# Attention scores as products of 64 rows, two at a time in the halves of the array

## Chip, cores and metric

The kernel runs on one core of a Trainium2 chip. The metric is the time of one execution on the device in microseconds (us); the median of three runs stands for a kernel. The span of a profiled execution is the time from its first to its last instruction.

## What is computed

Two layers on float32 inputs. The change touches the first layer's attention: 8 sequences of 512 tokens, width 256, 16 heads of 16.

```python
qkv = jnp.einsum('bsd,hde->bhse', x, Wqkv) + bqkv[None, :, None, :]   # x: layer norm of the input, (8, 512, 256)
q, k, v = jnp.split(qkv, 3, axis=-1)
score = jnp.einsum('bhsd,bhtd->bhst', q, k)
score = jnp.where(causal[None, None], score, -jnp.inf)
attn = jax.nn.softmax(score / jnp.sqrt(HEAD_DIM), axis=-1)
out = jnp.einsum('bhst,bhtd->bhsd', attn, v)   # then transposed to (b, s, d)
out = out @ Wout + bout
```

After it come a mixture of nine experts (one of them shared), a gated scan and a second mixture, which the change leaves as they are. Their weights and loops are not shown.

## The kernel before

`mix_phase` does the first attention and the router of the experts, one batch (a sequence, 512 tokens) after the other, 8 in all; `experts_phase` and `layer1_phase` follow it. Each engine has its own instruction list, in which waits on semaphores are written by hand: `pe` (TensorE), `dve` (VectorE), `act` (ScalarE), `pool` (GpSimd), and `sp` (SyncE, which issues nearly all DMAs). An engine works its list strictly in the order written, and a DMA that SP issues stands behind all waits that SP has before it.

**Precision.** Products are made of float16 parts: x is split into a high and a low part, and a product is hi*hi + hi*lo + lo*hi (`three_products`, L143). For the scores the three are stacked along the contraction: `q_stack` and `k_stack` (L197, L198) hold for each head 16 rows of (hi, hi), 16 of (hi, lo) and 16 of (lo, hi), in partitions 0 to 47. Rows 48 to 95 are zero (cleared once, `clear`), and row 96 holds minus the row's maximum on the q side and ones on the k side. The stacks are filled through DRAM: ACT and DVE make `qk_hi` and `qk_lo` with (head, dimension) on the partitions, SP stores them (L350, L359), and once they have landed fetches them back as 16 rows by heads (`fetch_heads`, L372 to L376, six DMAs of 128 KB a half batch). Two sets of stacks alternate by batch.

**Two passes over the scores.** The *q pass* (`scores_q`, L908) has a block of 128 queries on the output's partitions and the keys along it; a mask product (identity times `mask_qk`, L925) puts -1e30 above the diagonal; DVE reduces each unit to minus its row maximum (`maxima`, L752). A group is four heads; its work is cut into 11 units (`A_UNITS`, L78) of up to 512 columns, which go through two banks in turn. When a group is through, DVE turns its 128x32 block of maxima (`turn_maxima`, L761) and ACT sends it with four small DMAs into row 96 of `q_stack` (`load_max`, L540). The *k pass* (`scores_k`, L927) has keys on the partitions and queries along it, over 97 rows, so that the maximum comes off in the product; ACT takes the exponential (L537), POOL clears above the diagonal (L452), and the value products (L955, float32, four heads side by side in strips of 32 columns of the array) sum over keys.

**Order.** The loop over s (head 0 to 127 through all batches) and n (0 to 2) gives each engine one slot per (s, n). A slot of PE has: the k pass of head s+1 part n, one q unit of the group two ahead (`LEAD`), and in named slots other work: values, transposes, the projections of the next batch, the output projection of the last (`AT_...`, L90 to L95). The slot number within a batch is at = 3h + n (0 to 47), within a group i = at mod 12. The k pass of a group begins at i = 9 of the group before (s+1 is a multiple of 4 at i = 9) and waits for `max_loaded` (L933); the q units wait for `stacks_loaded` at at = 24 (first half of the next batch) and at = 0 (second half).

## Time and profile before

| | us |
|---|---|
| median of 3 timed runs | 1208.96 |
| lowest, highest | 1206.2, 1209.35 |
| span of the profiled execution | 1206.9 |
| attention stage (first q product of batch 0 to the last k products) | 28.8 to 446.5 |
| a batch in the middle of it | 51.44 |

The profile is of one execution. The page gives the totals of each engine; the views below cut the stretch of the attention out of it. TensorE's time has two kinds of row: PE (products; their ends are modelled, so the distance of two starts says more than a length) and PEld (weight loads).

### The profile page before, as it was taken

How to read it: one execution, taken by the hardware profiler on the slowest of the kernel's cores; microseconds unless marked ns; L12 is line 12 of the kernel's file. 1: busy time of each engine (PE TensorE's matmuls, PEld its weight loads, DVE VectorE, ACT ScalarE, POOL GpSimd, SP SyncE). 2: the span in 40 equal slices, each digit the busy share in tenths (PEclk: the TensorE clock that was granted, in tenths of full speed). 3: DMA queues.
4: the chain of work that ended last, by engine and by line, in shares of the span. 5: the costliest groups of instructions: out<-in, count | busy, mean ns of one | idle time of the engine just before them, and what ended most of it. 6: DMA issues, size and time to landing. Idle time of an engine off the chain costs nothing. (4 is left out here: it accounts for less than half of the span.)

```text
span 1206.9 us, 26712 instructions
## 1 busy us (share of the span) xinstructions
PE 1111.1 (92%) x8873; PEld 745.7 (62%) x8905; DVE 897.4 (74%) x2217; ACT 676.1 (56%) x1463; POOL 529.1 (44%) x743
## 2 busy tenths in 40 slices
PE   4789999999999987998999999996999999999998
PEld 2345555555455546887999888983656646546555
DVE  5778887888888757975766657775876877877876
ACT  2256565555556564565656656664654664664653
POOL 5443434334243235844444444423646547447414
PEclk9689999999999999999999999998999999999999
DMA  5538544354533404665232453452241331331211
GB/s 146 112 67 237 102 80 98 80 111 96 93 81 80 99 19 155 215 179 165 79 127 83 119 163 124 126 149 85 89 141 36 106 126 48 105 102 64 96 45 62
DMA packets 105044, 129.36 MB, mean 107 GB/s; under 512 B 14976, under 2 KB 92736, under 8 KB 103936
## 3 DMA queue, kind: packets, MB, share of 16 engines
q1 hardware_dynamic: 93952, 109.27, 33.8%
q0 software_dynamic: 6912, 18.88, 5.6%
q8 instruction: 46, 0.75, 0.3%
q10 hardware_dynamic: 4096, 0.14, 0.2%
q14 instruction: 38, 0.31, 0.1%
HBM read 84.70 MB, written 43.38 MB: 106 GB/s over the span
## 5 line engine op out<-in xcount | busy, mean ns | idle before, releaser
L537 ACT ACTIVATE p<-bank 128x384 f32<-128x384 f32 (+1 forms) x384 | 191.9, 530 | 186.4 <-PE bank L937 118.8
L757 DVE TENSOR_REDUCE neg_max<-bank 128x1 f16<-128x384 f32 (+3 forms) x352 | 219.7, 640 | 64.7 <-PE bank L925 56.4
L452 POOL TENSOR_SCALAR_AFFINE_SELECT p<-p 128x256 f32<-128x256 f32 x256 | 104.1, 410 | 247.3 <-ACT p L537 246.7
L922 PE MATMUL bank<-k_stack,q_stack 96*128 96x384 f16 (+3 forms) x512 | 133.5, 313 | 20.1 <-DVE neg_max L757 13.1
L1377 POOL DMA_INDIRECT fetched<-xn_dram,token_now x80 | 81.2, 1015 | 42.8 <-POOL token_now L1373 30.6
L937 PE MATMUL bank<-q_stack,k_stack 97*128 97x512 f16 (+1 forms) x256 | 91.5, 362 | 6.0 <-ACT p L537 3.5
L2006 POOL TENSOR_TENSOR up_lo<-up_sq,up_hi 128x512 f16<-128x512 f32 x32 | 43.9, 1399 | 120.7 <-ACT up_hi L2063 120.7
L2017 POOL TENSOR_TENSOR he_lo<-he_sq,he_hi 128x512 f16<-128x512 f32 x64 | 79.9, 1268 | 36.7 <-ACT he_hi L2106 36.6
L1461 ACT ACTIVATE a<-xbank,b 128x256 f32<-128x256 f32 (+1 forms) x126 | 58.6, 468 | 51.2 <-PE xbank L149 47.8
L1549 DVE TENSOR_TENSOR h_lo<-h,h_hi 128x256 f16<-128x256 f32 x159 | 68.4, 433 | 24.4 <-ACT h_hi L1470 23.5
L955 PE MATMUL bank<-p,v_aug 128*32 128x512 f32 (+3 forms) x1024 | 83.5, 445 | 0.8 <-DVE o_rows L737 0.8
L147 PE MATMUL ybank<-l_xT_hi,pack_hi 128*128 128x512 f16 x208 | 78.9, 379 | 4.9 <-DVE up_sq L2220 2.5
L922 PEld LDWEIGHTS bank<-k_stack,q_stack 96*128 96x128 f16 x512 | 45.0, 99 | 59.4 <-DVE neg_max L757 40.9
L1468 ACT ACTIVATE h<-prod 128x256 f32<-128x256 f32 x159 | 64.9, 408 | 26.3 <-DVE prod L1543 21.2
L149 PE MATMUL ybank<-l_xT_hi,pack_lo 128*128 128x512 f16 x208 | 78.8, 379 | 0.0
L148 PE MATMUL ybank<-l_xT_lo,pack_hi 128*128 128x512 f16 x208 | 78.8, 379 | 0.0
L925 PE MATMUL bank<-mask_qk,identb 128*128 128x128 bf16 (+1 forms) x321 | 76.9, 240 | 0.0
L1543 DVE SCALAR_TENSOR_TENSOR prod<-xbank,b,a 128x256 f32<-128x256 f32 (+1 forms) x126 | 58.4, 477 | 24.0 <-ACT a L1461 19.3
L147 PE MATMUL ybank<-pack_hi,up_hi 128*128 128x256 f16 x256 | 69.8, 273 | 0.0
L148 PE MATMUL ybank<-pack_lo,up_hi 128*128 128x256 f16 x256 | 69.8, 273 | 0.0
L149 PE MATMUL ybank<-pack_hi,up_lo 128*128 128x256 f16 x256 | 69.8, 273 | 0.0
L1991 POOL DMA_INDIRECT rows_k<-y_routed_dram,slot x56 | 56.5, 1008 | 27.7 <-issue 15.9
(342 smaller groups left out, 3375.2 us busy)
## 6 DMA issues: line engine op xcount, KB each, us to landing
w_bc<-wT_dram SPq DMA_DIRECT2D x8, 2048.0 KB, 8.0
y_routed_dram<-y SPq DMA_DIRECT2D x37, 256.0 KB
w<-in_w SPq DMA_DIRECT2D x10, 704.0 KB, 6.9
pack<-in_pack SPq DMA_DIRECT2D x12, 342.0 KB, 4.1
xr<-in_x SPq DMA_DIRECT2D x8, 512.0 KB, 7.3
xn_dram<-xn SPq DMA_DIRECT2D x8, 512.0 KB, 3.1
qk_hi_dram<-qk_hi SPq DMA_DIRECT2D x16, 256.0 KB, 2.4
qk_lo_dram<-qk_lo SPq DMA_DIRECT2D x16, 256.0 KB, 2.4
```

The costliest lines, as they stand in the source:

```text
L147: pe.matmul(out, hi_a(c), hi_b(c), start=first and x == 0, stop=False)
L148: pe.matmul(out, hi_a(c), lo_b(c), start=False, stop=False)
L149: mm = pe.matmul(out, lo_a(c), hi_b(c), start=False, stop=last and x == n - 1)
L452: pool.affine_select(out=diagonal, in_=diagonal, pattern=[[0, 2], [1, P]], compare_op=ALU.is_ge, fill=0.0, base=0, channel_multiplier=-1). ...
L537: act.activation(p32[:, s // GH % 2, s % GH, cols], s_bank[n][:, 0:cols.stop - cols.start], ACT.Exp).then_inc(p_exp.sem, 1)
L757: dve.tensor_reduce(neg_max[:, g % 2, 0:GH * TT].rearrange("p (h t) -> p h t", t=TT)[:, heads[0]:heads[-1] + 1, j], a_bank[c % 2][:, 0:len ...
L922: pe.matmul(to[:, at * w:(at + 1) * w], q_stack[0:STK, u, h0 + h, j * P:(j + 1) * P], k_stack[0:STK, u, h0 + h, 0:w], start=at == 0, stop= ...
L925: pe.matmul(diagonal, identb[:, :], mask_qk[:, 0:len(heads), :], start=False, stop=True).then_inc(a_psum.sem, 1)
L937: mm = pe.matmul(to[:, 0:S - n * P], k_stack[0:AUG, u, h, n * P:(n + 1) * P], q_stack[0:AUG, u, h, n * P:S], start=True, stop=True)
L955: mm = pe.matmul(out_bank[VW * h:VW * (h + 1), k * P:S], v_aug[:, b % 2, k, GH * (g % NG) + h, :], p32[:, g % 2, h, P_OFF[k]:P_OFF[k] + S ...
L1377: pool.indirect_dma_start(fetched[:, u, half, :], None, dram["xn"], bass.IndirectOffsetOnAxis(token_now[:, u, half:half + 1], 0)).then_inc ...
L2017: pool.tensor_tensor(he_lo[:, e, :], he_sq[:, e % EB, :], he_hi[:, e, :], ALU.subtract).then_inc(he_lo_s.sem, 1)
```

## The change

- The stacks have 48 rows (49 with the maximum) instead of 96 (97). Even heads stand in partitions 0 to 48, odd heads in 64 to 112; one tile column holds a pair of heads. The products of both passes so use the upper or the lower 64 rows. Clearing goes away; `free` holds the place of the memory saved.
- A q unit is of one parity (`par`) and one or two pairs. There are 12 units per group, one in each slot. In slot (s, n) the unit's parity is s mod 2 and that of the k pass is (s+1) mod 2.
- The mask is made of two products over 64 rows (`mask_rows`, `mask_cols`), one for each half of the 128 columns of a diagonal block, in the same rows of the array as the unit. POOL makes these masks in 13 small instructions at the start.
- DVE turns the maxima of a group one slot later, at i = 0, after that slot's reduction.
- SP sends the maxima, eight DMAs per group (four for each parity) instead of ACT's four; each has its place in SP's list, and the fetches, stores and loads behind it wait for it.
- DRAM holds the stacked order: SP stores each high part twice and each low part once (six DMAs of 128 KB a half batch, before two of 256 KB), and fetches 48 rows at once (four DMAs of 192 KB, before six of 128 KB).

```diff
-STK, AUG = 96, 97
+STK, AUG = 48, 49
+HI_SLOTS, LO_SLOTS = ((0, 2), (1, 2)), ((1,), (0,))
+HALF = 64
+HEAD_PAIRS = NH // 2
...
-A_UNITS = (((0, 1, 2, 3), 0), ((0, 1), 1), ((2, 3), 1), ((0,), 2), ((1,), 2), ((2,), 2), ((3,), 2),
-           ((0,), 3), ((1,), 3), ((2,), 3), ((3,), 3))
+A_UNITS = ((0, (0, 1), 1), (0, (0, 1), 0), (0, (0,), 2), (1, (0, 1), 1), (1, (0, 1), 0), (1, (0,), 2),
+           (0, (0,), 3), (0, (1,), 3), (0, (1,), 2), (1, (0,), 3), (1, (1,), 3), (1, (1,), 2))
...
-AT_MAX = {0: (0, 1), 1: (2, 3)}
...
-        q_stack = sb("q_stack", [AUG, 2, NH, S], F16)
-        k_stack = sb("k_stack", [AUG, 2, NH, S], F16)
+        q_stack = sb("q_stack", [P, 2, HEAD_PAIRS, S], F16)
+        k_stack = sb("k_stack", [P, 2, HEAD_PAIRS, S], F16)
+        free = sb("free", [P, 2, NH, S], F16)
...
+            def store_slots(of, half, places):
+
+                for a, slots in enumerate(places):
+                    for r in slots:
+                        to = dram["qk"][a, half * NH // 2:(half + 1) * NH // 2, r]
+                        sp.dma_start(to, of[:, 2 * a + half, :]).then_inc(qk_stored.sem, 16)
+
             def store_hi(b, half):
-                hi_rows = dram["qk_hi"].rearrange("(a m p) s -> p m a s", a=2, p=P)[:, half]
-                hi_tile = qk_hi[:, :, :].rearrange("p (a m) s -> p m a s", a=2)[:, half]
                 sp.wait_ge(qk_hi_s.sem, qk_hi_s.at(b, 2 * half + 2))
-                sp.dma_start(hi_rows, hi_tile).then_inc(qk_stored.sem, 16)
-
-            def load_stacks(b, half):
-
-                u, heads = b % 2, slice(half * NH // 2, (half + 1) * NH // 2)
-                lo_rows = dram["qk_lo"].rearrange("(a m p) s -> p m a s", a=2, p=P)[:, half]
-                lo_tile = qk_lo[:, :, :].rearrange("p (a m) s -> p m a s", a=2)[:, half]
+                store_slots(qk_hi, half, HI_SLOTS)
+
+            def store_lo(b, half):
                 sp.wait_ge(q_lo_s.sem, q_lo_s.at(b, half + 1))
                 sp.wait_ge(k_lo_s.sem, k_lo_s.at(b, half + 1))
-                sp.dma_start(lo_rows, lo_tile).then_inc(qk_stored.sem, 16)
+                store_slots(qk_lo, half, LO_SLOTS)
...
+            def load_max(g):
+
+                b, pair0 = g // NG, GH // 2 * (g % NG)
+                sp.wait_ge(max_rows_s.sem, max_rows_s.at(g))
+                for par in range(2):
+                    row = HALF * par + STK
+                    for q in range(4):
+                        to = q_stack[row:row + 1, b % 2, pair0:pair0 + GH // 2, :].rearrange("o h (t q c) -> o q h t c", t=TT, q=4)[:, q]
+                        at = 32 * q + GH // 2 * TT * par
+                        sp.dma_start(to.rearrange("o h t c -> o (h t) c"),
+                                     max_rows[at:at + GH // 2 * TT, g % 2, :]).then_inc(max_loaded[g % 2].sem, 16)
...
+            def fetch_heads(u, pairs, fetched):
+                heads = dram["qk"].rearrange("a (h w) r d s -> a w (r d) h s", w=2)
+                for par in range(2):
+                    for a, stack in enumerate((q_stack, k_stack)):
+                        sp.dma_start(stack[HALF * par:HALF * par + STK, u, pairs, :], heads[a, par, :, pairs, :]).then_inc(fetched.sem, 16)
...
             store_xn(0)
             load_x(1)
             for half in range(2):
                 store_hi(0, half)
+                store_lo(0, half)
                 load_stacks(0, half)
                 if half == 0:
                     store_xT(0)
             store_xn(1)
+            load_max(0)
             for b in range(NB):
                 if b + 2 < NB:
                     load_x(b + 2)
+                load_max(NG * b + 1)
                 if b + 1 < NB:
                     store_xT(b + 1)
                     store_hi(b + 1, 0)
+                    store_lo(b + 1, 0)
+                load_max(NG * b + 2)
                 if b + 1 < NB:
                     load_stacks(b + 1, 0)
+                load_max(NG * b + 3)
...
                     store_hi(b + 1, 1)
+                    store_lo(b + 1, 1)
+                    load_max(NG * b + 4)
                     load_stacks(b + 1, 1)
...
-            pool.wait_ge(w_lo.sem, 1)
-            clear(k_stack, 0)
+            make_masks()
...
-                        if i < AU:
-                            maxima(group(s), i)
-                        else:
-                            turn_maxima(group(s))
+                        maxima(group(s), i)
+                    if i == 0 and LEAD < group(s) <= GROUPS:
+                        turn_maxima(group(s) - 1)
...
-                heads, j = A_UNITS[i]
-                w = (j + 1) * P
-                for at, h in enumerate(heads):
-                    pe.matmul(to[:, at * w:(at + 1) * w], q_stack[0:STK, u, h0 + h, j * P:(j + 1) * P],
-                              k_stack[0:STK, u, h0 + h, 0:w], start=at == 0, stop=False)
-                diagonal = to[:, 0:len(heads) * w].rearrange("p (x w) -> p x w", w=w)[:, :, j * P:w]
-                pe.matmul(diagonal, identb[:, :], mask_qk[:, 0:len(heads), :], start=False, stop=True).then_inc(a_psum.sem, 1)
+                par, pairs, j = A_UNITS[i]
+                w, half, stack = (j + 1) * P, slice(HALF * par, HALF * par + HALF), slice(HALF * par, HALF * par + STK)
+                for at, h in enumerate(pairs):
+                    pe.matmul(to[:, at * w:(at + 1) * w], q_stack[stack, u, pair0 + h, j * P:(j + 1) * P],
+                              k_stack[stack, u, pair0 + h, 0:w], start=at == 0, stop=False)
+                blocks = to[:, 0:len(pairs) * w].rearrange("p (x w) -> p x w", w=w)
+                cols = mask_cols[half, 0:len(pairs), :]
+                pe.matmul(blocks[:, :, j * P:j * P + HALF], mask_rows[half, HALF:HALF + P], cols, start=False, stop=False)
+                pe.matmul(blocks[:, :, j * P + HALF:w], mask_rows[half, 0:P], cols, start=False, stop=True).then_inc(a_psum.sem, 1)
...
+                rows, pair = slice(HALF * (h % 2), HALF * (h % 2) + AUG), h // 2
                 if n < 2:
-                    mm = pe.matmul(to[:, 0:S - n * P], k_stack[0:AUG, u, h, n * P:(n + 1) * P], q_stack[0:AUG, u, h, n * P:S],
+                    mm = pe.matmul(to[:, 0:S - n * P], k_stack[rows, u, pair, n * P:(n + 1) * P], q_stack[rows, u, pair, n * P:S],
                                    start=True, stop=True)
...
-                "qk_hi": nc.dram_tensor("qk_hi_dram", (2 * D, S), F16).ap(),
-                "qk_lo": nc.dram_tensor("qk_lo_dram", (2 * D, S), F16).ap(),
+                "qk": nc.dram_tensor("qk_dram", (2, NH, 3, HD, S), F16).ap(),
```

## Rows read from the trace of the kernel before

**Rows 1.** Head of the page: span; busy us (share of the span) xinstructions.

```profile
span 1206.9 us, 26712 instructions
...
PE 1111.1 (92%) x8873; PEld 745.7 (62%) x8905; DVE 897.4 (74%) x2217; ACT 676.1 (56%) x1463; POOL 529.1 (44%) x743
```

**Rows 2.** Table of stretches: length, busy time (xinstructions) of each engine, clock, DMA share, GB/s.

```profile
160.19:211.63 51.44, 48.73 (x428) 27.80 (x430) 43.37 (x114) 30.51 (x65) 18.74 (x37) 1.00 0.48 93
...
412.00:446.80 34.80, 29.86 (x248) 14.91 (x250) 23.55 (x69) 22.67 (x49) 11.75 (x27) 0.95 0.05 17
29.35:53.25 23.90, 18.05 (x69) 6.66 (x70) 16.40 (x30) 2.38 (x5) 10.43 (x6) 0.50 0.64 125
53.25:66.90 13.65, 10.42 (x70) 5.52 (x69) 12.36 (x40) 8.19 (x17) 4.32 (x9) 1.00 0.26 78
```

**Rows 3.** Timeline of PE: start us, us, engine, line, operation, out<-in, shapes, count.

```profile
200.10 0.22 PE L925 MATMUL bank<-mask_qk,identb 128*128 128x128 bf16 x1
200.16 0.33 PE L937 MATMUL bank<-q_stack,k_stack 97*128 97x384 f16 x1
200.32 0.38 PE L922 MATMUL bank<-k_stack,q_stack 96*128 96x512 f16 x1
...
201.20 0.22 PE L925 MATMUL bank<-mask_qk,identb 128*128 128x128 bf16 x1
201.35 1.28 PE L955 MATMUL bank<-p,v_aug 128*32 128x384 f32 x16
202.57 0.39 PE L937 MATMUL bank<-q_stack,k_stack 97*128 97x512 f16 x1
...
205.05 0.60 PE L965 MATMUL bank<-identf,o_cols 128*128 128x128 f32 x4
205.48 0.60 PE L856 MATMUL bank<-identf,xn 128*128 128x128 f32 x4
```

**Rows 4.** Waits in the batch of 160.19 to 211.63: engine, line <- releaser: us, times, longest.

```profile
DVE neg_max L757 <- PE bank L925: 6.4, 9, 1.1
DVE xT_lo L643 <- ACT xT_hi L502: 0.6, 1, 0.6
...
PEld bank L922 <- DVE neg_max L757: 3.4, 9, 0.6
...
PEld bank L940 <- ACT p L537: 1.2, 2, 0.9
...
PEld bank L922 <- DMA k_stack<-qk_hi_dram: 0.4, 1, 0.4
```

**Rows 5.** Costliest groups of the page: value products (busy us, mean ns of one).

```profile
L955 PE MATMUL bank<-p,v_aug 128*32 128x512 f32 (+3 forms) x1024 | 83.5, 445 | 0.8 <-DVE o_rows L737 0.8
```

**Rows 6.** Groups by shape of DVE, 80 to 420 us: the row maxima.

```profile
L757 DVE TENSOR_REDUCE neg_max<-bank 128x1 f16<-128x512 f32 x108 | 73.5, 691 | 29.1 <-PE bank L925 28.0
L757 DVE TENSOR_REDUCE neg_max<-bank 128x1 f16<-128x384 f32 x108 | 59.0, 553 | 9.7 <-PE bank L925 9.2
```

**Rows 7.** Line 547, the sends of row maxima: min/median/max ns of an issue.

```profile
L547 ACTq DMA_DIRECT2D q_stack<-max_rows x128: 510/607/1955, 38.4 to 434.7; - x128
```

**Rows 8.** Timeline of ACT at the opening.

```profile
38.38 10.66 ACTq L547 DMA_DIRECT2D q_stack<-max_rows  x8
```

**Rows 9.** Timeline of SP's queue: first and last of six issues of one fetch.

```profile
169.96 0.32 SPq L375 DMA_DIRECT2D q_stack<-qk_hi_dram  x1
...
172.22 0.44 SPq L376 DMA_DIRECT2D k_stack<-qk_hi_dram  x1
```

**Rows 10.** Line 376, fetches of k_stack: us from issue to landing.

```profile
DMA to landing us min/median/max: 2.6/5.3/7.1
```

**Rows 11.** Table of stretches: a fetch of stacks, then a load of x.

```profile
144.00:152.00 8.00, 7.68 (x92) 4.20 (x91) 5.88 (x13) 3.87 (x9) 2.40 (x6) 1.00 0.94 114
152.00:154.00 2.00, 1.87 (x15) 1.08 (x15) 1.53 (x4) 1.84 (x5) 0.79 (x2) 1.00 0.84 209
```

**Rows 12.** Timeline of SP's queue: the issue behind the zeros.

```profile
96.33 10.75 SPq L315 DMA_DIRECT2D xr<-in_x  x1
```

More of the change, by code:

```diff
@@ L232, in mix_phase @@
         v_filled = sig("v_filled", 2)
-        stacks_cleared = [sig(f"stacks_cleared{u}", 2) for u in range(2)]
+        mask_made = sig("mask_made", 13)
         ones_filled = sig("ones_filled", 16 * 2)
@@ L250, in mix_phase @@
         k_lo_s = sig("k_lo_s", 2)
-        qk_stored = sig("qk_stored", 32)
-        stacks_loaded = [sig(f"stacks_loaded{h}", 96) for h in range(2)]
-        first_heads_loaded = sig("first_heads_loaded", 96)
+        qk_stored = sig("qk_stored", 16 * 6)
+        stacks_loaded = [sig(f"stacks_loaded{h}", 16 * 4) for h in range(2)]
+        first_heads_loaded = sig("first_heads_loaded", 16 * 4)
         v_psum = sig("v_psum", 2)
@@ L263, in mix_phase @@
         max_rows_s = sig("max_rows_s", 1)
-        max_loaded = [sig(f"max_loaded{k}", 16 * 4) for k in range(2)]
+        max_loaded = [sig(f"max_loaded{k}", 16 * 8) for k in range(2)]
         s_psum = sig("s_psum", U)
@@ L360, in load_stacks @@
+            def load_stacks(b, half):
+                u, pairs = b % 2, HEAD_PAIRS // 2
                 sp.wait_ge(qk_stored.sem, qk_stored.at(2 * b + half))
                 if b >= 2:
-                    sp.wait_ge(s_psum.sem, s_psum.at((b - 2) * NH + heads.stop - 1))
-                else:
-                    sp.wait_ge(stacks_cleared[b].sem, stacks_cleared[b].at(0))
-                if b == 0 and half == 0:
-                    fetch_heads(u, slice(0, GH), first_heads_loaded)
-                    fetch_heads(u, slice(GH, 2 * GH), stacks_loaded[half])
-                else:
-                    fetch_heads(u, heads, stacks_loaded[half])
@@ L372, in fetch_heads @@
-            def fetch_heads(u, heads, fetched):
-                hi, lo = (dram[k].rearrange("(a h d) s -> a d h s", a=2, d=HD)[:, :, heads, :] for k in ("qk_hi", "qk_lo"))
-                for r, (q, k) in enumerate(((hi, hi), (hi, lo), (lo, hi))):
-                    sp.dma_start(q_stack[HD * r:HD * r + HD, u, heads, :], q[0]).then_inc(fetched.sem, 16)
-                    sp.dma_start(k_stack[HD * r:HD * r + HD, u, heads, :], k[1]).then_inc(fetched.sem, 16)
+                    sp.wait_ge(s_psum.sem, s_psum.at((b - 2) * NH + (half + 1) * NH // 2 - 1))
@@ new lines, in load_stacks @@
+                if b == 0 and half == 0:
+                    fetch_heads(u, slice(0, GH // 2), first_heads_loaded)
+                    fetch_heads(u, slice(GH // 2, GH), stacks_loaded[half])
+                else:
+                    fetch_heads(u, slice(half * pairs, (half + 1) * pairs), stacks_loaded[half])
+            def fetch_heads(u, pairs, fetched):
[3 more added lines that the diff above has]
+                        sp.dma_start(stack[HALF * par:HALF * par + STK, u, pairs, :], heads[a, par, :, pairs, :]).then_inc(fetched.sem, 16)
@@ L378, in _ @@
             sp.wait_ge(filled.sem, filled.at(0))
-            for u in range(2):
-                sp.dma_start(k_stack[STK:AUG, u, :, :],
-                             ones16[STK:AUG, :].unsqueeze(1).to_broadcast([1, NH, S])).then_inc(ones_filled.sem, 16)
+            for par in range(2):
+                row = HALF * par + STK
+                sp.dma_start(k_stack[row:row + 1, :, :, :].rearrange("o u h s -> o (u h) s"),
+                             ones16[row:row + 1, :].unsqueeze(1).to_broadcast([1, 2 * HEAD_PAIRS, S])).then_inc(ones_filled.sem, 16)
@@ L571, in _ @@
             router_exp(0)
-            for g in range(LEAD):
-                load_max(g, range(4))
             for n in range(U):
@@ L581, in _ @@
                         exps(s + 1, n)
-                    if at % (U * GH) in AT_MAX and LEAD < group(s) <= GROUPS:
-                        load_max(group(s) - 1, AT_MAX[at % (U * GH)])
                     if s >= GH and at % (U * GH) == AT_COPY:
@@ L1009, in _ @@
                         scores_k(s + 1, n)
-                    if group(s) < GROUPS and i < AU:
+                    if group(s) < GROUPS:
                         scores_q(group(s), i)
@@ L1067, in _ @@
         def _(pool):
-            pool.memset(zeros[:, :, :], 0.0).then_inc(start, 1)
+            pool.memset(zeros[:, :], 0.0).then_inc(start, 1)
             pool.memset(onesf[:, :], 1.0).then_inc(start, 1)
```

73 lines of the change are left out of this document (39 added, 34 removed).

## The prediction

> **What bounds the kernel now.** I read the head of the page first: TensorE (PE) is busy for 92% of the span, VectorE (DVE) for 74% [rows 1]. That mixes two layers; the change touches the attention stage alone, which runs from 29 to about 447 us. So the next view is the table of stretches. One batch there, cut from one store of xT by SP to the next, lasts 51.44 us: PE busy 48.7, DVE 43.4, ACT 30.5, POOL 18.7 [rows 2]. A batch has 48 slots (16 heads by 3), so a slot is 1.07 us. Of six such batches (1 to 6) most of the result must come; batch 0 runs partly at half clock, and batch 7 has no next batch to prepare and is over in 34.80 us [rows 2].
>
> PE's busy time counts the modelled tails of matmuls, so I count its stream by starts. A 128-column product is followed after 0.06 us, one of 384 after 0.16 [rows 3]: columns / 2.4 GHz. Per batch the code issues 20,480 columns in the k pass, 20,480 in the q pass, 8,192 of masks (49,152, that is 20.5 us), 24,576 of projections (10.3 us), 32 fp32 transposes at 0.11 us (3.5; four start 0.43 us before the next four), and eight value blocks of 1.2 us (10.0) [rows 3]; with the short logits and rank products some 45 us of 51.4. The value block also shows what a change of array shape costs: 0.15 us from the start of a 0.06 us mask product to the first 128x32 one, so 0.09 us for the turn. The way back is dearer at most by a little: 16 products of 384 and 256 columns, four side by side at four passes, stream for 1.07 us, and the next score product starts after 1.22, 0.15 us more [rows 3]. The list of waits for this batch says where the rest is: DVE waits 6.4 us for PE's mask products (L925), the last product of each unit, PE's weight loads wait 3.4 us for DVE's maxima (L757) and 1.2 for ACT's exponentials [rows 4]. So PE is the bound with DVE close behind (45 against 43.4), and 6 us are lost where each waits for the other over two banks.
>
> **The change, part by part.**
>
> *Side by side, 8.5 us per batch off PE.* In slot (s, n) PE issues the k pass of head s+1 and behind it one q unit. Their parities are always opposite (the head's is (s+1) mod 2, the unit's s mod 2), so one sits in rows 0 to 63 and the other in 64 to 127, and they write different banks. A q unit with its masks has 512 to 768 columns, the k pass 384 or 512, so the k pass (20,480 columns, 8.5 us) can hide under the q unit. No row of before shows two halves of rows at once. The nearest is the value product: 1024 of them of 445 ns each, 456 us in all, take 83.5 us of busy time, since four heads share the array in 32-column strips [rows 5]. That is the upper end; the lower end is nothing. I take the whole, since that row is the same array divided the other way.
>
> *More instructions.* Masks become two products of 64 columns per head instead of one of 128: the same columns, 24 products per group against 11. Products with a weight load each follow at their columns' pace down to 128 columns [rows 3]; no row has 64, so the 64 products of 64 columns per batch cost nothing if that holds and 1.7 us if each takes the 0.055 of 128. I take nothing, since most of that would lie in PE's new slack. DVE gets a twelfth reduction per group: a reduction of 512 elements takes 691 ns, one of 384 takes 553 [rows 6], so 256 take about 415; a group goes from 7.04 to 7.19 us, a batch from 43.4 to 44.0.
>
> *More turns of the array.* Before, all but the value products use one shape, so 8 blocks make 16 turns. After, scores have 64 rows, projections and transposes 128, values 128x32. The slots with other work are 22 of 48, so some 45 turns. At 0.09 us [rows 3] 29 more cost 2.7 us per batch; between nothing (a turn that hides under a wait) and 0.15 us each (4.4), the way back. I take the way in, of which 0.09 is the clean reading. The Trainium skill, TensorEngine Tiling (Array Packing), Key Properties, says that a change of tiling mode drains the engine while tiles of one mode run independently. By its first half the added turns cost as above, by its second the k pass hides; a case in which only the first half held is the second rival.
>
> PE is then 45 - 8.5 + 2.7 = 39 us per batch, DVE 44.0: **the bound passes to DVE**. Its floor is 44.0 plus the 1.1 us of batch gaps that no wait explains (51.44 - 43.37 - 7.0 of waits [rows 2, 4]), 45.1. What PE still makes it wait is less than the 6.4 us of now, but not nothing: a slot with six 512-column products of a projection still takes PE 1.8 us, DVE 0.6 to 1.2. In the one stretch where PE was light (10.42 of 13.65), DVE was busy for 12.36 of 13.65 [rows 2], 91%; that would make 44.0 into 48.6. Between 45.1 and 48.6 I take 47.6, 3.8 us less than now.
>
> *ACT loses its sends.* Four per group at 607 ns, 9.7 us per batch, go to SP [rows 7]. ACT was busy 30.5 of 51.4, so that is slack, apart from part of the 2 us that PE waits for exponentials. In the opening it counts: eight sends hold ACT's queue from 38.38 to 49.04 [rows 8], the first exponentials stand behind the second four, which they don't need; of those some 2.6 us I count 1.5.
>
> *SP gets eight sends per group*, 32 per batch, and stores 6 instead of 2 tiles per half. An issue on SP takes 0.43 us and 0.05 to the next [rows 9], on ACT 0.6 [rows 7]; I take 0.55. SP's issues become 59 per batch, some 30 us of 47: it fits, but now fetches of the stacks queue behind a wait for maxima. Follow the second half: maxima of slot 36 are turned 1.3 us into it, 8 sends take 4.4, then four stack fetches, which slot 48 of PE needs. Before, a fetch took 7.6 us (the first half's: first issue at 169.96, last at 172.22, median landing 5.3) [rows 9, 10]. Its rate is 114 GB/s against 209 just behind it, where x goes to all 128 partitions [rows 11]. After, a fetch writes 48 partitions, not 16. The bounds are the old 7.6 us and 4.8 (768 KB at 209 GB/s and 1 us); I take 6. Then 1.3 + 4.4 + 6 = 11.7 us for 12 slots of 0.99 us: just in time, with no room. The Trainium skill, SBUF — State Buffer, Door 1: The DMA port swizzle, gives 27.2 GB/s per port; 16 partitions reach four of them (109 GB/s, which this trace agrees with), 48 reach eight. By that page's figures the fetch would be an estimated 5 us and the chain 10.7.
>
> *One collision.* In batch 0 SP writes 4 MB of zeros (L411), and its next issue, x, blocks for 10.75 us [rows 12]. On ACT's queue the maxima passed that by. Now the eight sends for batch 1 stand behind it: stacks of batch 1 go out some 2 us later than now, x is released near 106, the sends end near 110 and land near 113. PE needs them at slot 9 of batch 1. That batch begins near 103 now (51.44 before the one that begins 6 us ahead of 160.19) and near 99 then, so slot 9 is near 108, the start of batch 1 plus 9 slots of 0.99. **6 us lost, once.**
>
> *At nothing:* the 3.5 us clears of the stacks on DVE and POOL go (POOL, 18.8 of 51.4, and the opening of DVE have room), 13 small mask instructions come on POOL, done before the first stacks land near 28; the first store and fetch of stacks get some 2 us more of issue and a fetch two shorter.
>
> **Sum.** Batches 1 to 6: 6 x 3.8 = 23. Batch 0: 2.5. Batch 7: 3 (q units in its first half only; then exponentials set the pace). Opening: 1.5. Collision: -6. In all 24 off. The profiled execution has a span of 1206.9, the median of the timed runs is 1208.96, 2 above; the forecast is 1185 us, a span of 1183.
>
> **Rivals.**
> 1. *SP becomes the bound* (18%). If the fetch keeps its 7.6 us and a send costs 0.6, the chain is 1.3 + 5.2 + 7.6 = 14.1 us, twice per batch; with 24 other slots at 0.99 a batch lasts 52.0. Then +3.6 for six batches, -7 for batches 0, 7 and the opening, +6: 1211 us. Half-way cases give 1197 to 1211. For it: the chain has no room; PE already waits for stacks now and then (0.4 us in this batch) [rows 4]. Against: 48 partitions instead of 16.
> 2. *Slower: the turns are paid and nothing runs side by side* (14%). Each 64-row product then occupies PE as before: 45 + 2.7 = 47.7 us, with the 6 lost between the engines 53.8 per batch, 2.4 more. With six batches (+14), batches 0 and 7 (+3), the opening (-1.5) and part of the collision (hidden less, +3 to 6): about 1228. It decides from the point where less than 2.7 of the 8.5 us is hidden. A variant ends there too: the clock stood at half (1.2 GHz) from 29.35 to 53.25 with PE busy for 18.05 of 23.90, after it had waited for the first stacks [rows 2]; a PE idle for a fifth of each batch could see more of it.
> 3. *DVE alone sets the pace* (12%): batches at 45.5 and a collision of 4: 1169 us.
> 4. *The forecast* (53%): 1173 to 1197. The last 3% is for what I don't see.
>
> **Numbers.** A difference under 0.3% (3.6 us) is about what a measurement of this kernel can't tell from none. Faster: the forecast, the third rival and half of the first, 0.74; same: the other half of the first, 0.09; slower: 0.17. Leaving out 4% below and some 15% above, the range is 1168 to 1213.
>
> **What would show it.** Right: k and q products of one slot starting within some 10 ns of each other; DVE above 90% busy in a batch, PE's waits on DVE the longest of its list; a PE wait of some 5 to 6 us for max_rows near 108; stack fetches at 150 GB/s or more. Wrong: products of opposite halves spaced by their columns (rival 2); PE waits of over 1 us per batch on stacks or max_rows after batch 1 (rival 1); turns far from 0.09 us; clock below 1.00 in batches 1 to 6.

## The result: slower by 6%

The changed kernel takes 1285.93 us (median of 4, 1280.82 to 1291.07), the kernel before 1208.62 beside it: ratio 1.0645, 95% interval 1.061 to 1.068. The forecast was 1185, with a range of 1168 to 1213. Two single runs of the experiments below, 1568 us of nosend_light_free and 2866 us of before_nosend_light_free, stand far above the other runs of their kernels and are left out of their ratios.

The head of the profile after (engines, then the granted clock in 40 slices), against [rows 1]:

```profile
span 1278.1 us, 27782 instructions
PE 1128.7 (88%) x9320; PEld 754.0 (59%) x9321; DVE 899.2 (70%) x2248; ACT 674.2 (53%) x1463; POOL 523.4 (41%) x751
PEclk9588888899989789799999999999899999999999
```

The span grew by 71.2 us. I cut both profiles at the instruction that turns the maxima of a group (before L765, after L796), four a batch. Up to the fifth turn (opening and batch 0) it is 91.4 before and 96.7 after: +5.3. The next 24 turns, six batches, take 306.6 and 361.1: +54.5, or **+9.1 a batch where -3.8 was forecast**. To the last turn it is 34.6 and 41.1: +6.5. Behind it +4.9. The table of stretches for the six batches, before and then after (us; busy times; clock; DMA share; GB/s):

```profile
91.40:398.00 306.60, 291.93 (x2557) 166.33 (x2581) 256.35 (x667) 180.79 (x379) 108.90 (x220) 1.00 0.50 105
```

```profile
96.70:457.80 361.10, 300.84 (x2894) 169.22 (x2892) 260.03 (x691) 178.67 (x378) 108.00 (x220) 0.88 0.39 98
```

DVE's work is nearly what it was (256 and 260 us), ACT's too. No engine became the bound: PE is busy for 83% of the stretch, DVE for 72%. And the clock, 1.00 before, is 0.88: of these 361 us PE spent 85 at 1.2 GHz.

One batch of after, against [rows 4]. List of waits, 251.2 to 310.0 (us in total, times, longest):

```profile
DVE neg_max L789 <- PE bank L956: 13.6, 14, 3.4
PEld bank L951 <- DMA k_stack<-qk_dram: 6.8, 2, 3.4
PE bank L951 <- DMA k_stack<-qk_dram: 6.2, 2, 3.1
PEld bank L951 <- DVE neg_max L789: 6.0, 10, 0.8
PEld bank L969 <- DMA q_stack<-max_rows: 1.3, 1, 1.3
```

Twice a batch PE stands still for 3.1 us until a half of the stacks lands. Why it lands late is in the timeline of SP's queue (start, length of the issues, line, count):

```profile
249.17 2.48 SPq L354 DMA_DIRECT2D qk_dram<-qk_hi  x4
251.75 1.18 SPq L354 DMA_DIRECT2D qk_dram<-qk_lo  x2
252.98 5.39 SPq L374 DMA_DIRECT2D q_stack<-max_rows  x8
258.47 0.38 SPq L394 DMA_DIRECT2D q_stack<-qk_dram  x1
...
260.28 0.44 SPq L394 DMA_DIRECT2D k_stack<-qk_dram  x1
```

The maxima are turned at 251.2. SP is still issuing the six stores, begins the sends at 252.98, and issues the first fetch at 258.47. Before, the low parts' store was one issue of 0.36 us, and only its landing (1.8 us, 219.6 to 221.4) stood between it and the fetch; now the sends do, longer than a landing.

The side by side itself is there. PE's timeline, after:

```profile
245.59 0.40 PE L987 MATMUL bank<-p,v_aug 128*32 128x256 f32 x4
245.92 0.39 PE L969 MATMUL bank<-q_stack,k_stack 49*128 49x512 f16 x1
245.93 0.39 PE L951 MATMUL bank<-k_stack,q_stack 48*128 48x512 f16 x1
246.15 0.19 PE L955 MATMUL bank<-mask_cols,mask_rows 64*128 64x64 bf16 x1
246.19 0.19 PE L956 MATMUL bank<-mask_cols,mask_rows 64*128 64x64 bf16 x1
246.31 0.39 PE L149 MATMUL bank<-xT_hi,wqkv_hi 128*128 128x512 f16 x1
```

Two products of 512 columns start 0.01 us apart, the mask behind them 0.22 later: two passes for the time of one. From the last mask product (64 columns, 0.03 us) to the first over 128 rows it is 0.12, so 0.09 for the turn of the array.

### The profile page after: what moved, and what is told of

It is laid out like the page before. It is cut to its first block and busy times, and to the rows that moved or that the text cites. A ratio compares the mean times of both kernels' runs of the same rounds, so it can differ in the third digit from the quotient of the medians.

```text
span 1278.1 us, 27782 instructions
## 1 busy us (share of the span) xinstructions
PE 1128.7 (88%) x9320; PEld 754.0 (59%) x9321; DVE 899.2 (70%) x2248; ACT 674.2 (53%) x1463; POOL 523.4 (41%) x751
## 5 line engine op out<-in xcount | busy, mean ns | idle before, releaser
L789 DVE TENSOR_REDUCE neg_max<-bank 128x1 f16<-128x512 f32 (+3 forms) x384 | 224.5, 597 | 128.5 <-PE bank L956 125.4
L951 PE MATMUL bank<-k_stack,q_stack 48*128 48x384 f16 (+3 forms) x512 | 142.7, 344 | 77.8 <-DMA k_stack<-qk_dram 43.9
L951 PEld LDWEIGHTS bank<-k_stack,q_stack 48*128 48x128 f16 x512 | 43.6, 101 | 103.0 <-DVE neg_max L789 51.3
L969 PE MATMUL bank<-q_stack,k_stack 49*128 49x512 f16 (+1 forms) x256 | 94.1, 401 | 9.5 <-DMA q_stack<-max_rows 8.9
L987 PE MATMUL bank<-p,v_aug 128*32 128x512 f32 (+3 forms) x1024 | 94.3, 493 | 0.8 <-DVE o_rows L768 0.8
L1491 ACT ACTIVATE a<-xbank,b 128x256 f32<-128x256 f32 (+1 forms) x126 | 58.8, 469 | 52.0 <-PE xbank L151 48.5
L955 PE MATMUL bank<-mask_cols,mask_rows 64*128 64x64 bf16 (+1 forms) x384 | 84.9, 221 | 0.0
L956 PE MATMUL bank<-mask_cols,mask_rows 64*128 64x64 bf16 (+1 forms) x384 | 82.6, 215 | 0.0
```

Of the source, the lines that this page charges most:

```text
L789: dve.tensor_reduce(to, a_bank[c % 2][:, 0:len(pairs) * w].rearrange("p (x w) -> p x w", w=w), AX.X, ALU.max, negate=True).then_inc(a_max. ...
L951: pe.matmul(to[:, at * w:(at + 1) * w], q_stack[stack, u, pair0 + h, j * P:(j + 1) * P], k_stack[stack, u, pair0 + h, 0:w], start=at == 0, ...
L955: pe.matmul(blocks[:, :, j * P:j * P + HALF], mask_rows[half, HALF:HALF + P], cols, start=False, stop=False)
L956: pe.matmul(blocks[:, :, j * P + HALF:w], mask_rows[half, 0:P], cols, start=False, stop=True).then_inc(a_psum.sem, 1)
L969: mm = pe.matmul(to[:, 0:S - n * P], k_stack[rows, u, pair, n * P:(n + 1) * P], q_stack[rows, u, pair, n * P:S], start=True, stop=True)
L987: mm = pe.matmul(out_bank[VW * h:VW * (h + 1), k * P:S], v_aug[:, b % 2, k, GH * (g % NG) + h, :], p32[:, g % 2, h, P_OFF[k]:P_OFF[k] + S ...
```

## Experiments

All runs are in one table, so that each section can point at it. "Batch" is the mean of six, cut as above; "half clock" is how much of one batch the granted clock was at 1.2 GHz, summed from the trace's clock records. The kernel before took 1208 us in some groups of runs and 1246 to 1252 in others. Its two traces, before and before_again, agree within 1 us up to the end of the attention; the 35 us between them come from the 820th us on. The second has 29 us more at half clock there, which can make up at most 14 of the 35; the cause of the rest is open. So ratios (each against the kernel before in its own group) and batches are compared, not times. nosend, nosend_same, fetch_first and split_first rest on two runs each, before_again on one, the others on three to ten.

| kernel | ratio (95%) | batch us | half clock us per batch |
|---|---|---|---|
| before | 1 | 51.1 | 0 |
| before_again | (one run) | 51.1 | 0 |
| after | 1.0645 (1.061-1.068) | 60.2 | 14.2 |
| after_again | 1.0617 (1.0555-1.0678) | 60.8 | 14.8 |
| act8 | 1.0575 (1.0552-1.0599) | 60.3 | 13.1 |
| split | 1.0312 (1.0285-1.0339) | 55.9 | 8.5 |
| fetch_first | 1.0958 (1.0904-1.1011) | 66.7 | 22.8 |
| split_first | 1.0807 (1.0691-1.0924) | 64.2 | 18.2 |
| after_fill | 1.0538 (1.0506-1.0571) | 59.4 | 9.1 |
| before_sp | 1.0427 (1.0389-1.0464) | 58.6 | 6.8 |
| before_sp_fill | 1.0336 (1.0308-1.0364) | 57.6 | 1.1 |
| nosend | 1.0115 (1.0007-1.0222) | 53.0 | 3.4 |
| nosend_same | 1.0371 (1.0294-1.0448) | 57.1 | 7.4 |
| before_nosend | 0.9987 (0.9966-1.0008) | 50.9 | 0 |
| nosend_free | 1.0086 (1.0058-1.0115) | 51.6 | 2.3 |
| before_nosend_free | 0.9924 (0.9897-0.995) | 50.9 | 0 |
| nosend_light | 1.009 (1.006-1.012) | 53.9 | 8.0 |
| before_nosend_light | 0.98 (0.9752-0.9848) | 49.0 | 0 |
| nosend_light_free | 0.964 (0.9606-0.9674) | 45.5 | 0 |
| before_nosend_light_free | 0.9679 (0.9644-0.9714) | 47.4 | 0 |

Of the letters in the first four expectations, A holds that SP's order hides a real saving, B that the new passes themselves cost the time, C that without sends the two layouts come out even.

**No sends (nosend), and both passes in one half (nosend_same).** The eight sends and the waits for them are left out, and the row of maxima is zeros, so the maximum is not taken off in the products. nosend_same has the changed order of units too (the last four lines), so that both passes of a slot are in the same 64 rows.

```diff
-            load_max(0)
...
-                    pe.wait_ge(max_loaded[g % 2].sem, max_loaded[g % 2].at(g // 2))
...
+                sp.dma_start(q_stack[row:row + 1, :, :, :].rearrange("o u h s -> o (u h) s"),
+                             zeros_f[row:row + 1, :].bitcast(F16).unsqueeze(1).to_broadcast([1, 2 * HEAD_PAIRS, S])).then_inc(ones_filled.sem, 16)
...
-A_UNITS = ((0, (0, 1), 1), (0, (0, 1), 0), (0, (0,), 2), (1, (0, 1), 1), (1, (0, 1), 0), (1, (0,), 2),
-           (0, (0,), 3), (0, (1,), 3), (0, (1,), 2), (1, (0,), 3), (1, (1,), 3), (1, (1,), 2))
+A_UNITS = ((1, (0, 1), 1), (1, (0, 1), 0), (1, (0,), 2), (0, (0, 1), 1), (0, (0, 1), 0), (0, (0,), 2),
+           (1, (0,), 3), (1, (1,), 3), (1, (1,), 2), (0, (0,), 3), (0, (1,), 3), (0, (1,), 2))
```

> The changed kernel without the sends of row maxima: the maxima are still computed and turned, but the row of the stacks that should hold them is set to zero once, so the exponentials are taken of unshifted scores. Theory A (SP's sends make the stack fetches and themselves late, and the clock falls because PE stands idle then): batches of 46 to 48 us against 58.8 in the changed kernel, no PE wait on stacks over 0.5 us per batch, clock 1.00 in batches 1 to 6, time 1170 to 1180 us. Theory B (products of 64 rows keep the clock from rising whatever SP does): clock still under 0.95 in batches 1 to 6, time above 1230. Theory C (the turns of the array and the added products eat the gain): batches above 51, time near 1210 or more, clock 1.00.

> As nosend, but the q units take their parities in the other order, so that the k pass and the q unit of a slot are in the same half of the array; instructions, turns of the array and columns are the same. If running side by side is worth the 8.5 us per batch of PE's stream that I counted, PE needs 47 to 48 us per batch and a batch lasts 51 to 53, so 25 to 40 us more than nosend. If the overlap is worth nothing, because DVE sets the pace in both, the two agree within 5 us.

Without sends five of the six points go. But what is left is no faster than the kernel before (the interval of the ratio, 1.0007 to 1.0222, lies above 1); a batch wholly at full clock lasts 51.2 us (nosend, 319.2 to 370.4) against 51.4 [rows 2]. A's 46 to 48 were missed and B fell. C was near: over 51 us a batch, but with 3.4 us of half clock where it expected none. In one half instead of two, four groups at full clock took 14.4, 13.8, 14.5 and 11.5 us, 54.2 a batch: side by side is worth 3 us (54.2 against 51.2), and without it the layout would be slower than before by about that. The 25 to 40 us expected between the two kernels held (1297 against 1265, 32), the batch of 51 to 53 did not (57.1, with 7.4 at half clock).

**The fetch ahead of the sends (fetch_first), and the sends divided as well (split_first).** If only the order on SP were wrong, turning it round would help. The last two lines are those of split_first: SP sends the odd heads' maxima only, and ACT the even ones'.

```diff
-                load_max(NG * b + 2)
                 if b + 1 < NB:
                     load_stacks(b + 1, 0)
+                load_max(NG * b + 2)
...
-                for par in range(2):
+                for par in (1,):
```

> The changed kernel with one edit: SP issues the fetch of a half batch of stacks before the sends of maxima that stand ahead of it, in both places. Theory A: PE's waits on stacks (33.8 us from 100 to 480 us) fall under 5 us; its waits on maxima grow from 5 to 10 to 25, since those sends now stand behind the fetch's own wait for the stores; time 1215 to 1250. If the fetch itself (its rate) were what is late and not its place in the list, the waits on stacks stay above 20 us and the time within 10 us of 1286.

> As fetch_first, and ACT sends the even heads' maxima (four sends per group, in its slots 1 and 2), SP only the odd heads' four. Theory A: SP's list is some 11 us per batch shorter and both transfers are in time: batches of 47 to 49 us, clock 1.00, time 1175 to 1195 us. If ACT's 0.6 us per send now holds up the exponentials, its waits show as PE waits on ACT and the time is 1195 to 1215.

Both missed, and far. SP's timeline and PE's list of waits in fetch_first (120 to 480 us):

```profile
276.45 0.44 SPq L394 DMA_DIRECT2D k_stack<-qk_dram  x1
276.94 19.07 SPq L374 DMA_DIRECT2D q_stack<-max_rows  x16
```

```profile
PE bank L969 <- DMA q_stack<-max_rows: 54.8, 12, 6.6
```

The wait on the stacks is gone from the list; PE waits 55 us for the maxima instead, where after waited 30 for the stacks and 5 for the maxima over the same 360. The sends now stand behind the fetch and behind the 3.6 us in which SP waits for the stores to land. Each order makes the other transfer late.

**Where the sends are issued (act8, split, before_sp).** Three kernels and a second look at after. act8 is in the diff: all eight sends on ACT, none on SP. split has the first two entries of the table, for the even heads, and leaves the odd ones on SP. before_sp is the kernel before with its four sends taken off ACT and put into SP's list at after's places.

```diff
+AT_MAX = {1: ((0, 0), (0, 1)), 2: ((0, 2), (0, 3)), 3: ((1, 0), (1, 1)), 4: ((1, 2), (1, 3))}
...
+                    if at % (U * GH) in AT_MAX and LEAD <= group(s) <= GROUPS:
+                        send_max(group(s) - 1, AT_MAX[at % (U * GH)])
```

> The changed kernel, unchanged, on the chip of this group: eight sends a group stand on SP. Every theory expects a ratio near that of the first measurement, 1.055 to 1.068, batches of 57 to 60 us and the longest wait of the product engine the one on the stacks.

> The changed kernel with its eight sends a group issued by ScalarE again, two a unit in the first four units of a group; nothing of them on SP. Theory Q (the loss is the stack fetch standing behind the sends in SP's order): ratio 1.00 to 1.02, as without sends (1.0115), stack waits of TensorE under 4 us a batch. Theory R (eight sends delay the maxima themselves, wherever they are issued): ratio 1.04 or more, waits on the row maxima take the place of those on the stacks.

> The changed kernel with the even heads' four sends on ScalarE and the odd heads' four on SP, in SP's old places: half of the 5.4 us stays before the fetch. Theory Q: between act8 and after_again, ratio 1.02 to 1.045. Theory R: equal to act8 and after_again, 1.04 or more.

> The kernel before with its four sends a group taken off ScalarE and put on SP at the places where the changed kernel has its eight: about 2.7 us and the wait for the maxima before each fetch. Theory Q: slower than before by 1 to 4%, waits on the stacks appear at the slots behind a fetch. If SP's order has cover enough in the old layout (theory S: only the new layout is hurt, since its fetch is larger and its slots shorter): ratio 0.995 to 1.005.

before_sp is the clean case: the old kernel and one part of the change. It loses 4.3%, and its trace shows the same thing as after. SP's queue, then PE's list (205.9 to 267.1, one batch of 61.2 us):

```profile
178.23 2.41 SPq L379 DMA_DIRECT2D q_stack<-max_rows  x4
180.74 0.53 SPq L359 DMA_DIRECT2D qk_lo_dram<-qk_lo  x1
183.05 0.33 SPq L384 DMA_DIRECT2D q_stack<-qk_hi_dram  x1
```

```profile
PE bank L923 <- DMA k_stack<-qk_hi_dram: 5.8, 2, 3.2
```

Here the low parts' store stands behind the sends too, and its landing behind that. S fell: the old layout had no cover either. Q had the mechanism for before_sp and just missed its size (1 to 4% expected, 4.3 found, interval 3.9 to 4.6). For split its number held (1.02 to 1.045, found 1.031) and its order did not: split was to lie between act8 and after_again and lies below both. SP's queue shows why half of the sends cost it so little. In nosend nothing stands between the stores and the fetch, and yet 3.1 us pass until they have landed; in split the four sends fill that time. Nosend, then split:

```profile
333.52 1.19 SPq L354 DMA_DIRECT2D qk_dram<-qk_lo  x2
337.83 0.33 SPq L394 DMA_DIRECT2D q_stack<-qk_dram  x1
```

```profile
295.00 1.25 SPq L355 DMA_DIRECT2D qk_dram<-qk_lo  x2
296.30 2.93 SPq L375 DMA_DIRECT2D q_stack<-max_rows  x4
299.33 0.42 SPq L395 DMA_DIRECT2D q_stack<-qk_dram  x1
```

From the last store issue to the first fetch it is 2.7 to 3.6 us in most half batches of nosend, 2.9 to 4.0 in split and 5.5 to 6.9 in after. So four sends behind the stores delay the fetch by some tenths of a us, eight by 2.4 or more. PE's waits on the stacks go with it: 8.2, 14.1 and 30.2 us over 360.

For act8 Q failed and R held. Its stacks are in time (0.6 us of wait in 360), but PE's list and ACT's, 120 to 480 us, say:

```profile
PE bank L979 <- DMA q_stack<-max_rows: 16.1, 10, 3.3
```

```profile
ACT p L581 <- issue: 14.7, 20, 1.9
```

Two sends (1.3 us) stand ahead of an exponential in each of four slots, and the eight of a group are spread over 4 to 6.5 us. Four sends are free on ACT (before_nosend against before: 0.9987); eight cost on SP and on ACT. That is a cost of the layout, which doubles the sends because each parity has a row of its own. after_again repeated the first measurement (1.0617 within the 1.055 to 1.068 expected, its batch of 60.8 just above the 57 to 60).

**Is it the clock?** Twelve idle products of 512 columns keep PE busy ahead of each wait on the stacks, 2.6 us at full clock. They write the bank that the real scores overwrite, and PE's wait for that bank moves ahead of them.

```diff
+                    if b >= 1:
+                        for _ in range(FILL):
+                            pe.matmul(to[:, 0:S], wqkv_hi[:, 0, 0:P], wqkv_hi[:, 0, 0:S], start=True, stop=True)
                     pe.wait_ge(stacks_loaded[half].sem, stacks_loaded[half].at(b))
```

> The changed kernel; before each of the 14 waits for the stacks from batch 1 on TensorE does 12 idle products of 512 columns into the bank that the real scores overwrite (2.6 us at full clock), so it is not idle while the stacks arrive. Theory G (the clock falls because TensorE stands still, and half of the loss is that clock; 112 of the 440 us of its window phase were at half clock, 3 in the kernel before): half-clock time in the window phase falls to under 60 us, ratio 1.02 to 1.045. Theory H (the waits cost only their own length and the half clock is not a cost of its own): ratio 1.06 or more, since work was added.

> The kernel before with its sends on SP and the same 12 idle products before each wait for the stacks. Theory G: half-clock time in the window phase falls from 58 to under 20 us, ratio 1.02 to 1.035 where before_sp had 1.043. Theory H: 1.04 to 1.05.

G's numbers hold in the old layout (half clock between the 75th and the 500th us from 58 to 10 us, ratio 1.034) and not in the new (75 to 515 us: 116 to 82, where under 60 was expected; 1.054 where 1.02 to 1.045 was). H fell: 36 us of useless products (14 times 12 at 0.213) made both kernels faster, though in after the two intervals overlap by a little. So the half clock is a cost of its own. In the six batches of before_sp 34 us less of it gave 6 us. How large it is in all stays open: the 6 are what was left after the idle products' own time, and in half of the places the next product follows them within 0.2 to 0.5 us, so there they may well last longer than the wait that they cover.

**What the passes are worth when nothing else binds.** The sends are left out in all of these. `light`: DVE's maxima read a quarter of their columns (they are not used), some 15 us a batch off DVE. `free`: from batch 1 on the stacks are fetched from what batch 0 stored, ahead of the stores, which go to a spare tensor; all scores are then batch 0's.

```diff
-                                  a_bank[c % 2][:, 0:len(pairs) * w].rearrange("p (x w) -> p x w", w=w), AX.X,
+                                  a_bank[c % 2][:, 0:len(pairs) * w].rearrange("p (x w) -> p x w", w=w)[:, :, 0:w // 4], AX.X,
...
-                        to = dram["qk"][a, half * NH // 2:(half + 1) * NH // 2, r]
+                        to = dram["qk" if b == 0 else "qk_spare"][a, half * NH // 2:(half + 1) * NH // 2, r]
```

> The kernel before, unchanged, for its profile on the chip of this group. Every theory expects batches of about 51.4 us in the window phase, clock 1.00 from batch 1 on, waits of PE on the stacks under 4 us a batch.

> The kernel before without its 14 row-maximum sends; the row of negated maxima is zeros instead, so the maximum is no longer taken off in the products and nothing waits for it. Theory X (the side by side passes are worth about 3 us of a batch and the turns of the array take most of it back, so both layouts without sends are about equal): 1190 to 1208 of a kernel before at 1208, ratio 0.985 to 1.000, batch 50 to 51.4 us. Theory Y (the sends cost the kernel before several us a batch too, and the new layout is really slower): ratio under 0.98, batch under 49.5.

> As the last, and the row-maximum reductions on VectorE read only a quarter of their columns (the maxima are not used), so VectorE gives up about 14 to 16 us a batch. If VectorE and the buffers that it frees set the pace (theory D): batch 46 to 48 us, since TensorE's 45 to 48 us stay, ratio 0.93 to 0.96. If TensorE alone bounds (theory T): 50 us a batch, ratio 0.98 to 1.00.

> The changed kernel without sends and with the reductions reading a quarter of their columns, as the last. Theory D (TensorE's saving was real but VectorE's 43.8 us of 51.2 and its place in the loop hid it): batch 41 to 45 us, that is 3 us or more under the kernel before made light the same way, ratio 0.88 to 0.93. Theory T (the side by side saves about what the turns of the array cost): the two light kernels are within 1.5% of each other, batch 46 to 50 us.

> The changed kernel without sends, and with the stacks' round trip through memory cut: from batch 1 on the projections' results are stored to a spare tensor, and the stacks are fetched from those of batch 0 (so all scores are batch 0's), ahead of the stores. VectorE's work is whole. The prediction's core number is tested here: it gave TensorE 39 us and VectorE 44.0 a batch and a batch of 47.6, ratio to before 0.97 to 0.985. Theory K (the stores and the fetch, and the half clock behind their waits, hid the gain): batch 46 to 48.5 us. Theory L (TensorE and VectorE wait for each other over two banks, and the turns and the shorter overlap eat the gain): batch 50 to 51.5 us, ratio 0.99 to 1.01.

> The kernel before without sends and with the same round trip cut (stacks of batch 0 for all batches, stores to spare tensors). Both theories expect nearly no gain, since its waits on the stacks were under 1 us a batch: ratio 0.985 to 1.00, batch 50.5 to 51.4 us.

> nosend_free with the row-maximum reductions reading a quarter of their columns: neither VectorE, nor sends, nor the stacks can bind. Theory K: batch 39 to 43 us, ratio 0.92 to 0.95, and at least 4 us a batch under its counterpart of the old layout. Theory L or a smaller saving on TensorE: 44 to 47 us, within 2 us a batch of the counterpart.

> The old layout's counterpart of the last: batches of 46.5 to 48.5 us (TensorE's stream of some 45 us and little else), ratio 0.965 to 0.98.

before_again was as expected in the attention (51.1 us a batch, no half clock in the six batches). X held (0.9987, batch 50.9); before_nosend_light came out between D and T (49.0 us, 0.98). nosend_light is the instructive miss, by both theories. With 15 us less for DVE the new layout got no faster (53.0 to 53.9 us a batch), because PE then ran ahead of the stacks. Its list of waits, 120 to 480 us:

```profile
DVE neg_max L786 <- PE bank L952: 139.3, 117, 4.3
PEld bank L947 <- DMA k_stack<-qk_dram: 37.3, 12, 4.5
```

With the stacks out of the way as well, the comparison is clean; all these batches are at clock 1.00. The table of stretches, a whole batch and its group with the least other work, old layout, then new:

```profile
208.40:255.70 47.30, 46.69 (x428) 28.20 (x431) 28.60 (x115) 29.93 (x64) 18.90 (x37) 1.00 0.53 102
221.00:231.40 10.40, 10.34 (x118) 6.49 (x116) 5.05 (x18) 6.17 (x15) 3.17 (x8) 1.00 0.95 158
```

```profile
207.90:253.60 45.70, 43.66 (x485) 25.32 (x484) 28.93 (x119) 29.53 (x63) 18.72 (x38) 1.00 0.45 117
220.40:229.80 9.40, 9.10 (x128) 5.96 (x128) 4.38 (x19) 5.74 (x15) 2.87 (x9) 1.00 0.74 188
```

**The new layout is worth 1.9 us a batch (47.4 to 45.5), with PE nearly alone as the bound.** Half of it is in one of the four groups. The array changes its shape 45 times in the batch of nosend_light_free and 16 times in that of the old layout: the 29 more turns of the prediction. At 0.09 us they take 2.6, so by difference the side by side saves 4.5 and not 8.5. K's 39 to 43 were missed; the smaller-saving branch (44 to 47, within 2 us) held, and so did what was expected of the old layout (46.5 to 48.5, 0.965 to 0.98).

With DVE whole (nosend_free) even the 1.9 is gone. Its groups at full clock last 13.5, 13.5, 13.1 and 10.8 us, 50.9 a batch; those of before_nosend_free 13.1, 13.3, 13.4 and 11.2, 51.0. K fell. L's ratio held, and its batch of 50 to 51.5 holds at full clock (with the half clock the mean is 51.6); the old layout was within what was expected of it. Table of stretches, nosend_free, then before_nosend_free:

```profile
300.00:351.00 51.00, 44.73 (x485) 25.33 (x483) 43.71 (x118) 29.49 (x63) 18.55 (x38) 1.00 0.43 104
```

```profile
300.00:351.00 51.00, 48.27 (x429) 27.81 (x431) 43.45 (x114) 29.96 (x65) 18.68 (x37) 1.00 0.47 84
```

PE is busy 3.5 us less, and the batch is as long. Lists of waits, 120 to 420 us, nosend_free, then before_nosend_free:

```profile
DVE neg_max L789 <- PE bank L955: 43.1, 62, 2.4
PE bank L950 <- DVE neg_max L789: 32.2, 64, 1.0
```

```profile
DVE neg_max L763 <- PE bank L930: 40.6, 56, 1.2
PE bank L927 <- DVE neg_max L763: 10.5, 26, 0.5
```

PE waits 22 us more for DVE's maxima, 3.7 a batch, which is all that it saved; and DVE still waits for PE's mask products as long as before. The two take turns at waiting.

## Why the prediction was wrong

*Side by side takes 8.5 us off PE:* the mechanism was right (and the second rival fell): products start together, as the prediction's own check asked for. The size was not: 4.5 with nothing else in the way (a difference, as above; no row shows it alone), 3 with DVE whole. It counted columns as if the k pass always had a partner streaming. The starts show the exception: in nosend_light_free k products of 512 and 384 columns pair off within 3 ns, and then 0.3 us, in one slot 0.9, pass before the next q unit, the longer one a wait for DVE to empty the bank.

*More turns, 29 at 0.09 us, 2.7 us:* right in number and price.

*Masks and the twelfth reduction at nothing:* right as far as it shows; masks follow at 0.03 to 0.04 us, DVE's busy time went from 43.4 to 44.1 a batch, the 0.6 forecast.

*The bound passes to DVE, 47.6 us a batch:* **the first step that failed.** DVE's floor was taken from its sum over a batch. But PE and DVE hand each other two banks, so what PE gains in one slot it can lose in the next, waiting for DVE. The starts of the k passes show this (mean of batches 1 to 6, nosend_free against before_nosend_free): 23 of the 48 slots are shorter, most by 0.2 to 0.3 us and 5.9 in all, 20 of them without other work; the other 25 are 6.6 us longer, while PE's waits for DVE go from 1.6 to 5.3 a batch (2.3 us of half clock are in these sums). With DVE made light, 25 slots give 5.9, and the others take only 4.0, of which some 2.6 are the turns. By groups at full clock it is 11.2 to 10.8 us in the one with little other work, 13.1 to 13.5 in the one behind it. The trace of before had said so: DVE busy 43.4 of 51.4 and yet waiting 6.4 for PE [rows 2, 4], PE's loads waiting 3.4 for DVE. I read that as a loss that PE's slack would lift. The Trainium skill, TensorEngine Tiling (Array Packing), PSUM Bottleneck, warns that tiling speeds up TensorE but not the emptying of its banks. These runs agree: 0.1 us a batch with DVE whole, 1.9 with DVE made light.

*SP's chain of 11.7 us, "just in time, with no room":* **the second, and the one that turned the sign.** From the turn of the maxima to the landing of the fetch it had 4.4 + 6 = 10.4 us. Measured: 1.7 in which SP still issued stores (the six tiles were counted as a total, not at their place ahead of the sends), 5.5 for the sends (0.67 us each, taken at 0.55), 1.8 to the last fetch issue and 4.6 to its landing, 13.6 in all. That is 3.2 too late, and 3.1 is what PE waits in the list above, twice a batch. Of the 3.2 too many, 1.7 are the stores, 1.1 the price of a send, 0.4 the fetch. The first rival had this chain nearly right (14.1 with its 1.3 ahead, so 12.8), in part by luck: it left out the stores too and took 7.6 for a fetch of 6.4. It had only 18% and 1211 us, since it kept the saving on the other slots, which wasn't there.

*Clock:* it stood as a variant of the second rival for "a PE idle for a fifth of each batch". 1.2 GHz for 14 of 60 us came with two waits of 3 us and the shorter ones. It became less as waits went away: without sends 3.4 us a batch, with the stacks free as well 2.3, with DVE light too none.

*ACT loses its sends:* right, and worth nothing (before_nosend 0.9987). But the opening, forecast 1.5 us shorter, was 1.5 longer to the first turn (38.1, then 39.6), ahead of any send, and 1.4 longer to the first exponential (49.1, then 50.5), which without sends starts at 46.7 and 46.8: the sends on SP held it up more than those on ACT had.

*The collision behind the zeros, 6 us:* it is there. By the prediction's own times (landing near 113, needed near 108) it would have been 5. From the sixth turn to the seventh it is 13.4 us before, 15.5 in nosend and 19.3 in after: about 4 by the sends alone, and PE waits 3.0 us for the maxima there, not 5 to 6. (A smaller slip: eight value blocks of 1.2 us are 9.6 us of PE, not 10.0.)

**The sum, as measured.** Per batch: sends 5 points of the 6 (1.0617 less 1.0115; in batches 60.8 less 53.0), half clock within that; the rest is the new layout, even at full clock and 2.1 us a batch slower with its own half clock and some late stacks (nosend 53.0 against 50.9).

**Open.** Why nosend_free, in which PE waits for no transfer from the 120th to the 420th us, still sees 2.3 us of half clock a batch where the old layout sees none. It is open, too, how much of the 9 us a batch the half clock makes. And what a layout with side by side passes but four sends would do was not tried; by nosend, which has none and took 1.0115, it could hardly come out better than even. No version ran faster than the kernel before with its full result.

## What to carry to other kernels

Where two engines hand each other small banks, don't price a saving from sums over a batch: follow it from slot to slot and ask whether the next slot only waits longer. A step moved onto an in-order queue costs its own issue time to everything behind it and inherits everything ahead of it: write down the queue's order with times, down to the last landing, and if the result is "just in time", forecast it as late. Issues that fit into a landing for which the queue waits anyway cost little (split); those beyond it cost in full. An engine's waits of 3 us can cost more than 3 us when its clock falls behind them.

## What was new about the hardware

- Products over opposite halves of the rows start as little as 3 ns apart, each with columns of its own, and turns between 64-row, 128-row and 128x32 shapes all cost 0.09 to 0.10 us. In nosend_light_free a product over 128 rows starts 0.146 us after a 64-row one of 128 columns (0.053 us), a 128x32 one 0.116 after a 64-row one of 64 columns (0.027), and a 64-row one 0.205 after a 128x32 one of 0.107.
- A send of half a KB holds SP for 0.67 us (5.39 for eight), one of 1 KB for 0.60 (2.41 for four), a fetch of 192 KB for 0.44. In these rows the smaller transfer has the longer issue.
- Useless products ahead of a wait made the kernel faster (1.0427 to 1.0336), with 10 us at half clock where there had been 58.
